# Both halves of a batch's probability-value products in one PSUM bank

## The reference, cut to what matters

```
q, k, v = layernorm(x) @ Wq.T + bq, ctx @ Wk.T + bk, ctx @ Wv.T + bv
scores  = einsum('bgrqd,bgkd->bgrqk', q, k) / sqrt(8), masked with -inf
w       = softmax(scores)
out     = einsum('bgrqk,bgkd->bgrqd', w, v)      # the products of this change
x = x + tanh(g0) * (out @ Wo.T + bo)
x = x + tanh(g1) * moe(layernorm(x))             # silu(gate) * up, down, combined by the router
```

## Time and profile before

| | |
|---|---|
| median of 3 runs | 269.31 us (268.87 to 269.36) |
| span of the profiled execution | 267.6 us |
| PE busy | 237.8 us, 89% |
| DVE busy | 188.0 us, 70% |
| ACT busy | 96.7 us, 36% |
| POOL busy | 90.8 us, 34% |
| mean granted PE clock | 0.959 |

### The profile page before, as it was taken

The page is one execution under the profiler, slowest core; times in us unless marked ns, Lnnn a source line. Parts: engine busy times, 40 slices in busy tenths (PEclk is TensorE's granted clock), DMA queues, the critical chain, the costliest instruction groups (busy, mean ns, idle before and its releaser), DMA issues.

```text
span 267.6 us, 3780 instructions
## 1 busy us (share of the span) xinstructions
PE 237.8 (89%) x1275; PEld 168.9 (63%) x1275; DVE 188.0 (70%) x388; ACT 96.7 (36%) x173; POOL 90.8 (34%) x103
## 2 busy tenths in 40 slices
PE   0874889897789999999968999989999999999993
PEld 0751345454546555556544588768888888888883
DVE  2689786958877777675793377769767665766565
ACT  1575023857746565564546521111111010101000
POOL 6266008030081417361160110406936633562000
PEclk9997556999999999999999999999999999999998
DMA  7945400001100000211011000001322102000004
GB/s 208 159 129 127 109 1 2 0 0 43 39 0 1 2 0 7 55 21 37 1 26 35 1 2 0 0 0 39 82 61 60 38 21 61 0 0 2 0 0 158
DMA packets 20595, 10.25 MB, mean 38 GB/s; under 512 B 14400, under 2 KB 20064, under 8 KB 20576
## 3 DMA queue, kind: packets, MB, share of 16 engines
q1 hardware_dynamic: 20272, 9.79, 15.5%
q10 hardware_dynamic: 304, 0.22, 0.3%
HBM read 7.91 MB, written 1.05 MB: 33 GB/s over the span
## 4 chain that ended last, share of the span: by engine, by line
PE 74%; DVE 14%; ACT 5%; issue 3%; DMA 2%; ACTq 0%; DVEq 0%
PE bank L878 66%; ACT q L527 3%; PE bank L939 2%; DMA wkv_n<-in_L_xattn_Wv 2%; DVE q L629 2%; PE bank L918 2%; DVE mneg L740 2%; PE bank L935 1%; DVE xn L620 1%; DVE x_sb L871 1%; DVE w L782 1%; PE bank L952 1%; DVE xT L626 1%; PE bank L944 1%; DVE k L629 1%
## 5 line engine op out<-in xcount | busy, mean ns | idle before, releaser
L878 PE MATMUL bank<-xT,cT 128*128 128x512 f32 x288 | 70.2, 392 | 0.0
L878 PEld LDWEIGHTS bank<-xT,cT 128*128 128x128 f32 x288 | 53.7, 188 | 12.0 <-issue 0.8
L740 DVE TENSOR_REDUCE mneg<-bank 128x4 f32<-128x512 f32 x64 | 43.7, 687 | 19.6 <-PE bank L878 18.9
L585 ACT ACTIVATE pT<-bank 128x512 f32<-128x512 f32 x64 | 38.3, 601 | 28.4 <-PE bank L878 27.3
L572 ACT ACTIVATE pT<-bank 128x512 f32<-128x512 f32 x24 | 14.4, 598 | 84.2 <-PE bank L878 84.2
L878 PEld LDWEIGHTS bank<-w_d,q 128*128 128x128 f32 x288 | 37.1, 188 | 2.8 <-issue 1.3
L878 PE MATMUL bank<-q,kz 112*128 112x512 f32 x64 | 38.8, 609 | 0.0
L878 PE MATMUL bank<-w_d,q 128*128 128x256 f32 x288 | 38.0, 281 | 0.8 <-DVE q L818 0.8
L878 PE MATMUL bank<-kz,q 96*128 96x512 f32 x64 | 30.6, 484 | 5.9 <-DVE mneg L740 3.2
L411 POOL TENSOR_TENSOR vare<-mv,cst 128x1 f32<-128x1 f32 (+1 forms) x10 | 1.9, 194 | 82.4 <-DVE mv L614 80.4
L878 PE MATMUL bank<-cmask,ident_b 128*128 128x512 bf16 x64 | 28.4, 444 | 0.0
(11 more groups left out here) (119 smaller groups left out, 312.0 us busy)
## 6 DMA issues: line engine op xcount, KB each, us to landing
padf<-in_L_ffn_down_w SPq DMA_DIRECT2D x12, 128.0 KB, 2.3
c_sb<-in_ctx SPq DMA_DIRECT2D x2, 512.0 KB, 7.3
q<-q SPq DMA_DIRECT2D x8, 128.0 KB, 2.4
out<-x_sb SPq DMA_DIRECT2D x4, 256.0 KB, 2.4
c_sb<-in_L_ffn_gate_w SPq DMA_DIRECT2D x8, 96.0 KB, 2.2
c_sb<-in_L_ffn_up_w SPq DMA_DIRECT2D x8, 96.0 KB, 2.2
x_sb<-in_x SPq DMA_DIRECT2D x2, 256.0 KB, 3.6
x_sb<-in_x SPq DMA_DIRECT2D x1, 512.0 KB, 8.0
```

The costliest lines, as they stand in the source:

```text
L585: nc.scalar.activation(pT[:, i // 4, i % 4, :], bank[2 + s % 2][:], ACT.Exp, scale=SCALE).then_inc(p_done, 1)
L740: nc.vector.tensor_reduce(mneg[:, r, 4 * hf:4 * hf + 4], bank[n % 2][:].rearrange("p (g k) -> p g k", g=4), X, ALU.max, negate=True).then_ ...
L878: return nc.tensor.matmul(dst, a, b, start=start, stop=stop, skip_group_check=True)
```

## The change

`weigh_values` writes both halves to bank 4. Its second argument no longer names groups 0 to 3 or 4 to 7 but even or odd groups. The even groups' values stay in columns 0 to 8 of the 32, the odd ones' go to columns 16 to 24, and the odd products are added onto the even ones (start only in the first call, stop in the second), so that 32 partitions hold two groups. The slots of a batch take the groups in the order 0, 2, 4, 6, 1, 3, 5, 7. One copy, one TO job of four transposes and one reciprocal and product (of twice the width) a batch remain; the first copy (slot 8b+6) and the first TO (slot 8b+7) are gone. Bank 5, now free, joins banks 6 and 7 for jobs until slot 65. Two small instructions become two each: the memset of the ones and the copy of job vn. With three banks the early jobs take: kv(1) 7, x(1,0) 5, MT(1) 6, x(1,1) 7, wo 5, q(1,0) 6, TO(0) 7, q(1,1) 5, AT(0) 6, MT(2) 7, WO(0) 5; and later CT(0) follows AT(5) in bank 7 (before: WO(5) in bank 6).

```diff
+def group_of(i):
+    return 2 * (i % 4) + i // 4
...
-            at = {0: (7, 10, 13, 15, 18, 19), NB - 1: (7, 9, 10, 12, 14, 15)}.get(b, (7, 10, 12, 14, 18, 19))
-            for j, k in zip((("TO", b, 0), ("TO", b, 1), ("AT", b), ("WO", b), None, ("YT", b)), at):
+            at = {0: (10, 13, 15, 18, 19), NB - 1: (9, 10, 12, 14, 15)}.get(b, (10, 12, 14, 18, 19))
+            for j, k in zip((("TO", b), ("AT", b), ("WO", b), None, ("YT", b)), at):
...
-        BANK = {j: 2 + n % 6 if n < NA else 6 + n % 2 for n, j in enumerate(JOBS)}
+        def bank_of(n, j):
+            if n < NA:
+                return 2 + n % 6
+            return 5 + n % 3 if AT_SLOT.get(j, SLOTS) < FIRST_Y - 2 else 6 + n % 2
...
-            pool.memset(vz[:, :, :, HD:HD + 1], 1.0)
+            for sub in range(2):
+                pool.memset(vz[:, :, sub::2, 16 * sub + HD:16 * sub + HD + 1], 1.0)
...
-                nc.scalar.copy(o_sb[:, hf], bank[4 + hf][:]).then_inc(o_ok, 1)
+                nc.scalar.copy(o_sb[:], bank[4][:]).then_inc(o_ok, 1)
...
-                if s % G == 6 and s < CH:
-                    copy_o(s // G, 0)
                 if s % G == 1 and G < s < CH + G:
-                    copy_o(s // G - 1, 1)
+                    copy_o(s // G - 1)
...
-                    ins = nc.vector.tensor_copy(vz[:, j[1] * TPH:(j[1] + 1) * TPH, :, 0:HD],
-                                                ps[:, 0:TPH * 64].rearrange("p (b g d) -> p b g d", b=TPH, g=G))
+                    for sub in range(2):
+                        ins = nc.vector.tensor_copy(
+                            vz[:, j[1] * TPH:(j[1] + 1) * TPH, sub::2, 16 * sub:16 * sub + HD],
+                            ps[:, 0:TPH * 64].rearrange("p (b g d) -> p b g d", b=TPH, g=G)[:, :, sub::2])
...
-                    own(nc.vector.reciprocal(rden[:, hf], v[:, :, :, HD]))
+                    own(nc.vector.reciprocal(rden[:], v[:, :, :, HD]))
                     settle()
-                    a = an[:, 4 * hf:4 * hf + 4].rearrange("p j r d -> p r j d")
-                    ins = nc.vector.tensor_tensor(a, v[:, :, :, 0:HD], rden[:, hf].unsqueeze(3).to_broadcast([P, R, 4, HD]),
-                                                  ALU.mult)
+                    ins = nc.vector.tensor_tensor(an[:].rearrange("p g r d -> p r g d"), v[:, :, :, 0:HD],
+                                                  rden[:].unsqueeze(3).to_broadcast([P, R, G, HD]), ALU.mult)
...
-                b, g = n // G, n % G
+                b, g = n // G, group_of(n % G)
...
-            def weigh_values(b, hf):
-                pe.wait_ge(p_done, G * b + 4 * hf + 4)
-                if b:
-                    pe.wait_ge(o_ok, 2 * (b - 1) + hf + 1)
+            def weigh_values(b, sub):
+                pe.wait_ge(p_done, G * b + 4 * sub + 4)
+                if b and sub == 0:
+                    pe.wait_ge(o_ok, b)
                 for j in range(4):
-                    ins = mm(bank[4 + hf][VW * j:VW * (j + 1), :], vz[:, b, 4 * hf + j], pT[:, hf, j], True, True)
+                    ins = mm(bank[4][VW * j:VW * (j + 1), :], vz[:, b, 2 * j + sub], pT[:, sub, j], sub == 0, sub == 1)
```

More of the change, by code:

```diff
@@ L143, in build @@
         pT = sb("pT", [P, 2, G // 2, R * L])
-        o_sb = sb("o_sb", [P, 2, R * L])
-        rden = sb("rden", [P, 2, R, G // 2])
+        o_sb = sb("o_sb", [P, R * L])
+        rden = sb("rden", [P, R, G])
         an = sb("an", [P, G, R, HD])
@@ L296, in emptied @@
             return job_lo, ln[j] + 1
-        BANK = {j: 2 + n % 6 if n < NA else 6 + n % 2 for n, j in enumerate(JOBS)}
+        FIRST_Y = min(s for n, s in DOWN_SLOT.items())
+        def bank_of(n, j):
+            if n < NA:
+                return 2 + n % 6
+            return 5 + n % 3 if AT_SLOT.get(j, SLOTS) < FIRST_Y - 2 else 6 + n % 2
+        BANK = {j: bank_of(n, j) for n, j in enumerate(JOBS)}
+        LAST5 = [j for j in JOBS if BANK[j] == 5][-1]
         def jbank(j):
@@ L559, in _, with copy_o @@
             high(("MT", 0))
-            def copy_o(b, hf):
-                sc.wait_ge(pv_done, 2 * b + hf + 1)
+            def copy_o(b):
+                sc.wait_ge(pv_done, 2 * b + 2)
                 if b:
-                    sc.wait_ge(job_done, jn["TO", b - 1, hf] + 1)
-                nc.scalar.copy(o_sb[:, hf], bank[4 + hf][:]).then_inc(o_ok, 1)
+                    sc.wait_ge(job_done, jn["TO", b - 1] + 1)
+                nc.scalar.copy(o_sb[:], bank[4][:]).then_inc(o_ok, 1)
             def silu(n):
@@ L672, in take @@
                 elif k == "TO":
-                    _, b, hf = j
-                    v = ps[:].rearrange("p (r j c) -> p r j c", r=R, c=VW)
+                    b = j[1]
+                    v = ps[:].rearrange("p (r g c) -> p r g c", r=R, c=VW // 2)
                     if b:
-                        ve.wait_ge(*emptied(("TO", b - 1, hf)))
+                        ve.wait_ge(*emptied(("TO", b - 1)))
                         ve.wait_ge(job_done, jn["AT", b - 1] + 1)
-                    own(nc.vector.reciprocal(rden[:, hf], v[:, :, :, HD]))
+                    own(nc.vector.reciprocal(rden[:], v[:, :, :, HD]))
                     settle()
-                    a = an[:, 4 * hf:4 * hf + 4].rearrange("p j r d -> p r j d")
-                    ins = nc.vector.tensor_tensor(a, v[:, :, :, 0:HD], rden[:, hf].unsqueeze(3).to_broadcast([P, R, 4, HD]),
-                                                  ALU.mult)
+                    ins = nc.vector.tensor_tensor(an[:].rearrange("p g r d -> p r g d"), v[:, :, :, 0:HD],
+                                                  rden[:].unsqueeze(3).to_broadcast([P, R, G, HD]), ALU.mult)
                 elif k == "AT":
@@ L936, in job @@
                 elif k == "TO":
-                    pe.wait_ge(o_ok, 2 * j[1] + j[2] + 1)
+                    pe.wait_ge(o_ok, j[1] + 1)
                     for r in range(R):
-                        ins = nc.tensor.transpose(ps[:, r * P:(r + 1) * P], o_sb[:, j[2], r * L:(r + 1) * L], ident)
+                        ins = nc.tensor.transpose(ps[:, r * P:(r + 1) * P], o_sb[:, r * L:(r + 1) * L], ident)
                 elif k == "AT":
-                    pe.wait_ge(*emptied(("TO", j[1], 1)))
+                    pe.wait_ge(*emptied(("TO", j[1])))
                     a = an[:].rearrange("p g r d -> p (g r d)")
@@ L1033, in down @@
                     pe.wait_ge(p_done, CH)
-                    pe.wait_ge(o_ok, 2 * NB)
+                if h and ORDER[n - 1][1] == 0 and t == 0:
+                    pe.wait_ge(o_ok, NB)
+                    pe.wait_ge(*emptied(LAST5))
                 for u in range(TPH):
```

## The result

The changed kernel takes 268.23 us (median of 14 runs, 266.12 to 268.70) where the kernel before takes 269.28 on the same chip (14 runs, 268.27 to 269.67): ratio 0.9949, 95% interval 0.993 to 0.9968. It is faster by 1.05 us, a quarter of the 4.06 forecast, and outside the range. The profiled execution took 268.69 us, the second longest of the 14, with a span of 266.9, so 0.7 less than the span before. What follows first accounts for that 0.7, slot by slot; it is the account of one execution of each kernel.

A forecast was written before the change was run, and what follows sets the result against it. PE was taken to set the pace from 80 to 132.4 us, with other engines holding it up from 49.5 to 80. The terms 2.3 + 1.76 + 0.15 − 0.15 = 4.06 us gave about 265.2 us, range 263.6 to 267.2.

The forecast's parts named there:

- Slots 9 to 16: Slots 9 to 16: q(1,1) and MT(2) stop waiting, WO(0) hangs on AT(0)'s take and starts at 69.55, 2.34 us earlier.
- slots 18 and 19: Before YT(0): POOL's memset still precedes and holds batch 0's normalisation, so YT(0) starts 2.3 us earlier, not 2.78.
- adding of odd onto even products: Products accumulated in one bank, every batch: price taken as 0, at most eight times 0.1 us.
- The third bank: Slots 5 to 8: bank waits go, gaining 0.76 us, with TO(0,0)'s 0.44 together 1.20 at the end of slot 8.
- The wider pair: DVE's reciprocal and product of twice the width: 0.69 us instead of 0.54, costing 0.15 where PE waits behind it.
- three signs that the prediction named against itself: Wrong if slot 8b+8 exceeds 2.02 us, WO(0) starts after 70.5, or the granted clock dips after slot 4.
- I let it count in full: PE follows only itself in these slots.: Regular batches: the TO jobs removed in slots 23, 31, 39 and 47 save 4 x 0.44 = 1.76 us.
- Rival 3: Slower: PE's clock falls in the wait before YT(0); with ten slots at the low clock, 273.1 us; chance 0.04.
- the TO of slot 55: Slots 51 to 55: removing this TO was put at no gain, as PE waited 0.89 us behind it.
- rival 1: Slots 18 and 19: the normalisation overtakes the memset, YT(0) comes 1.4 us earlier still, 263.8 us; chance 0.17.
- rival 4: No measurable change: products in one bank cost 0.8 us or more a pair, or two rivals meet; 269 us; chance 0.03.
- Rival 2: Third bank buys little, as DVE and ACT hold the early slots; 2.05 us remain, 267.2 us; chance 0.11.

The follow-up runs named there:

- run 4: Changed kernel with its jobs after the first 13 in banks 6 and 7 only, as before the change: 269.56 us, ratio 1.001 to the kernel before.
- Run 1: Changed kernel, POOL's expert weight splits in batches 3 to 5 waiting for DVE's normalisation of the batch before: 266.31 us, ratio 0.9901.
- run 3: Changed kernel with 8 needless matmuls into idle bank 0 in slot 55, ahead of CT(0): 266.32 us, ratio 0.9898.
- run 9: The changed kernel itself measured once more, as a yardstick: 268.81 us, ratio 0.9968 to the kernel before.
- run 3b: The same kernel as run 3, measured a second time: 266.48 us, ratio 0.9898.
- run 2: Changed kernel with POOL's large memset, its neighbours and its wait for q(1,1) moved a batch earlier: 269.38 us, ratio 1.0016.
- run 10: Changed kernel with POOL's bias addition in eight pieces, batch by batch, instead of one instruction: 263.9 us, ratio 0.9796.
- Run 13: Changed kernel with 8 needless matmuls in slot 55 and 10 more in slot 5: 266.84 us, ratio 0.9904.
- run 11: Changed kernel with bias addition in eight pieces, weight splits and memset later, and 8 needless matmuls in slot 55: 260.76 us, ratio 0.9663.
- run 12: Kernel before the change with bias addition in eight pieces, weight splits and memset later, without needless matmuls: 263.66 us, ratio 0.9799.
- run 5: Changed kernel with POOL's whole bias addition moved behind DVE's normalisation of the second half of x: 270.35 us, ratio 1.004.

## Why the prediction was wrong, by its own steps

**Right.** *Slots 9 to 16* (1.52 for the 1.58 that remain when slot 9 is the origin; the changed kernel's MT(2) and q(1,1) without a wait), *slots 18 and 19* (the order of memset and normalisation, the 2.00 us, the wait of 1.39), and the *adding of odd onto even products* at 0 (slot 40: 2.00 us). Also the 0.44 for one TO (0.45 measured) and CT(0) behind c2. *The third bank* is the part of the change that pays: run 4 shows that without it nothing is left after what the clock takes. *The wider pair* was put 0.08 too low (0.77 for 0.69), by the reciprocal, 0.35 instead of 0.27: its price was taken from the product's 1.0 ns an element, and 16 elements more cost it 98 ns. That is the size of a term, and small. Of the three signs that the prediction named against itself two came: the clock dips after slot 4, and WO(0) starts at 70.74, later than 70.5; slot 8b+8 did not get longer.

**The step that failed in the regular batches:** "I let it count in full: PE follows only itself in these slots." PE does follow itself at the four TOs, but YT(2) in slot 35 hangs on a run of work on POOL that starts, with WO(2) in slot 30, ahead of the removed TO, and then goes at POOL's pace: the split holds the normalisation, and so PE. Of the four TOs two were given back there. Run 1 shows it: with the split behind the normalisation the slots are 0.73 shorter each, and nothing is given back. The busy shares could not show it, since PE was at 52.21 of 52.40 us; the normalisation's 0.70 us in that place, against 0.40 where it is alone, was in the trace of before and was the sign.

**The step that failed in slots 5 to 8** is not the rotation: at an undiminished clock the stretch gave 1.10 (runs 1 and 3: 10.15 and 10.16 us against 11.25; 1.20 was forecast). What failed is that it was costed at full clock. In the changed kernel's profile, and in runs 9, 3b and 2 the clock fell there, and the stretch took 11.13, 11.05, 11.07 and 11.00. So the dip costs about 0.9 us of this stretch in an execution where it occurs. It came with PE's wait of 3.24 us in all four, and not with 3.03 and 3.04 (runs 1 and 3). Length alone does not decide it: in other places the clock fell around waits of 1.92 to 2.39 us (slot 55) and 2.07 (YT(0) in run 10). What does decide it stays open, and so does its share in the medians: run 3 without the dip and run 3b with it took 266.39 and 266.50 in their profiled executions, as 3b was earlier at row maximum 15 by 0.81. It is not even shown to be the change's own. The kernel before has the same bias addition, and of its 79 executions on record with a clock beside the experiments 39 have a mean granted clock of 0.974 or 0.975 and 20 one of 0.968 to 0.971. One fall of 3.3 us to half the clock is 0.006 of the span, so part of these 20 may have it as well; that is an estimate, which no profile tests. Run 13, which was to settle the matter, did not.

**Rival 3 named the right mechanism in the wrong place.** It was given 0.04 and looked only at YT(0), where the clock stayed up after 1.39 us. The pauses that counted were the one in slot 5 and the one in front of CT(0). For the second the prediction had the parts. It says that the TO of slot 55 "is worth nothing: PE waited 0.89 behind it", and with the 0.72 in front and the 0.63 of the TO itself the pause without it comes to 2.2 us, near the 2.43 of the earlier trace rows. That step, a term put at nothing, is the one that cost most: to remove the TO cost 1.20 us, and run 3 puts needless work in its place and gets that back. The reading of the earlier trace rows was not exact either: the clock was down by 24 us, inside the wait that ended at 24.67, and another of 2.72 had ended at 21.07. The rival as a whole did not happen: the kernel is not slower. Nor did rivals 1 and 4: the memset kept its place ahead of the normalisation, and the products cost nothing.

**Was the sum sound otherwise?** Runs 11 and 12 are the nearest answer, the change made in surroundings without POOL's holds, and with the pause filled: 2.90 us by medians, up to 4.35 by slots. The forecast was 4.06, and its own terms without the memset's hold (2.78 in place of 2.3) make 4.54. The forecast counted pieces of PE's work about rightly and missed what stood around them. Rival 2's price of 2.05 comes nearer to the measured 1.05, but its reason does not hold: the third bank bought 0.68 of 0.76 in slots 5 to 8 (run 4) and what it was to buy from slot 9 on.

## What to carry to other kernels

Before a piece taken from the pacing engine is counted in full, list every later wait of that engine and ask of each chain behind it whether it starts at the engine's own pace; where it hangs on another queue, as YT(2) on POOL's split, the gain is given back there. Work that "only fills a pause" can hold the clock up: ask how long PE stands still without it, and compare with pauses in the trace around which the clock fell. As the length of one wait did not settle it here, fill the pause with needless work once and look. And where one engine's long instruction holds another, cutting it into pieces (run 10: 4.9 us) beat moving it (runs 2 and 5: slower than the changed kernel).

## What was unexpected of the hardware

- Eight matmuls of no use, 1.90 us of PE's time, made the kernel 1.4 to 1.9 us faster by the ratios (run 3).
- One GpSimd instruction of 4.55 us held a DVE instruction of 0.19 us for 4.53 (run 5).
- The granted clock comes back from its first fall at a different time in each execution: at about 31.5 and 36 us in two of one kernel (runs 3b and 3), at about 35.5 in the changed kernel's and 44.2 in that of the kernel before. The last two then start slot 5 at 44.02 and 47.21, and these 3.19 us are worth nothing here as long as the bias addition sets row maximum 15.
- The clock fell around waits of 2.07 to 2.39 us and stayed up through waits of 3.03 and 3.04 (runs 10, 1 and 3).
